# The phasor attention phase: output tile begun with three of four units, and the surplus matrix built in halves behind the phases

## The chip, the cores and the metric

The program runs on one core of one Trainium2 chip. The metric is device time of one execution in microseconds (us), lower is better. The kernel before takes 3089.39 us (median of three runs, 3087.33 to 3092.5).

## The reference, cut to what matters

The whole layer is attention of one kind (A), a feed-forward block (F), attention of another kind (B) and the same feed-forward block, each added to its input. The change touches only the first, on `x` of 8 rows, 1024 tokens, 256 features:

```python
x = x + attn_a(layernorm(x), Wk, Wv, Wo, gate, freqs)

def attn_a(x, Wk, Wv, Wo, gate, freqs):            # H, D = 16, 64; HD = 1024
    k_real = (x @ Wk).reshape(B, T, H, D)
    v = (x @ Wv).reshape(B, T, H, D).astype(complex64)
    k = exp(1j * (k_real * 10.0))
    rotors = exp(1j * (t[:, None, None] * freqs))[None]
    out_pos = real(cumsum(v * rotors, axis=1) * conj(rotors)) / sqrt(t + 1)
    k_shifted = roll(k, 1, axis=1).at[:, 0].set(0.0)
    out_assoc = real(cumsum(v * conj(k_shifted), axis=1) * k) / sqrt(t + 1)
    out = out_pos * gate[:, 0] + out_assoc * gate[:, 1]
    return out.reshape(B, T, HD) @ Wo
```

## The kernel before, in words

`build_layer` runs four phases one after the other, each in a block of its own with a barrier between: A, F, B, F. Only `phase_a` is changed. It walks over 8 batch rows (a "pass" each, the first and the last unrolled, the others in a loop), and in each over 8 **units** c = 0..7, a unit being 128 of the 1024 hidden features for all 1024 tokens. Units are numbered n = 8b + c through the phase.

Each engine has its own instruction list, written by hand, and runs it in order. Semaphores join them. For a unit n the work is:

- **TensorE** (PE) computes the phases' argument `u` (`project_u`, L627, 8 matmul records into `a_pu`) and `v` in two halves (`project_v`, L635, 4 records each into `a_pv`). An fp32 matmul is two records. It works ahead: in slot n it makes v of unit n+1 and u of unit n+2.
- **ScalarE** (ACT) in `front`: rounds u (L523, out `a_rnd`), then takes abs and two sines of the fraction (L525, L530, L531).
- **VectorE** (DVE) in `step`, 11 passes over the unit: products (L403 `even`, L408 `odd`), four scans (L414, L415), turns (L434, L444) and `fraction(n+1)` (L355), which needs the next unit's L523.
- **GpSimd** (POOL) in `post`, five passes (L268, L271, L277, L282, L285) that put the unit into `a_out[:, c]`; the last one signals `unit_done`. After units 1 and 2 it also makes the next row's means and scales.
- **TensorE** again, `project_out` (L658): 4 units are a **half row** of the hidden features. When units 0 to 3 are there, the four slots c = 4..7 each make two output tiles of 128 tokens, from a diagonal matmul with x (L670), for the first two slots two matmuls with the surplus matrix `fold` (L672), and four matmuls with `a_out` (L674). Units 4 to 7 are multiplied in slots c = 0..3 of the next pass. Before each pair it waits for `unit_done` of all four units. ScalarE scales the two tiles into `a_xr` (L538), SyncE stores them and loads the next row's x.

The order inside a TensorE slot is: first half of v, `project_out`, second half of v, u of unit n+2. So whatever `project_out` waits for, the second half of v and u wait too, and VectorE's L408 and L355 behind them.

The **surplus matrix** `fold` is needed since the scans run over pairs of neighbouring tokens: the sum of the earlier token of a pair holds the later one's term too. What is too much is linear in that token's x, and is added back with the opposite sign through a fixed 256x256 product of Wv, a scale per feature (`kap`) and Wo. It is built once, in the first pass, by `correction`: in slot 2 TensorE transposes `wv` (L648) in four groups into `a_py` and `a_pt`, ScalarE copies them scaled (L547, 8 copies) into the upper half of `a_out`; in slot 3 TensorE multiplies by `wo` (L655, 32 records) and ScalarE copies the two results (L551). On ScalarE, `correction(c)` stands ahead of `front` in its slot; ScalarE's other work there is sums of squares for the next row (`token_vars`, L497, 8 in slot 2) and normalising (L507).

```python
                def batch(b, first=False, last=False):     # ScalarE
                    for c in range(NC):
                        if first:
                            correction(c)
                        if not (last and c == NC - 1):
                            front(NC * b + c + 1, (c + 1) % NC, used=c >= 1 or not first)
```

## Time and profile before

| what | value |
|---|---|
| median of 3 runs | 3089.39 us (3087.33 to 3092.5) |
| the profiled execution | 3088.43 us, of which the span is 3086.6 us |
| mean granted TensorE clock | 0.961 of full |
| busy over the span: PE, DVE, ACT, POOL | 89%, 61%, 65%, 42% |
| phase A | from 0 to about 935 us |
| feed-forward 1, attention B, feed-forward 2 | to about 1560, 2480, 3087 us |

The span is what the profiler covers from the first to the last instruction. A row of the time line says when a group of instructions begins, how long it lasts, the engine, the line, output and inputs, how many there are, and in square brackets how long the engine was idle before it and what ended that. Since each engine runs in order, idle time of the engine that is busy nearly all of a phase is what a change can take away; idle time of another one costs only where its work is late for the first.

### The profile page before, as it was taken

Reading aid. Unit: us, or ns where it says so; the run is one execution under the profiler, and the core shown is the slowest. Engines: PE = TensorE matmul, PEld = TensorE weight load, DVE = VectorE, ACT = ScalarE, POOL = GpSimd, SP = SyncE. Lnnn points to the kernel's source line nnn. Section 1 sums busy time; section 2 is a strip of 40 time slices with the busy share of each in tenths; the row PEclk is TensorE's granted clock in tenths of the full one; section 3 lists DMA queues with packets and bytes.
Section 4 is the critical chain, followed back from the end, with each engine's and each line's share of the span. In section 5 each row is a group of like instructions: output and inputs, shape, how many; then the busy total and the mean of one; then the engine's idle time right before and its main releaser. Section 6 shows DMA issues by size and latency. Waiting matters only on the chain. (4 is left out here: it accounts for less than half of the span.)

```text
span 3086.6 us, 56032 instructions
## 1 busy us (share of the span) xinstructions
PE 2737.3 (89%) x20897; PEld 1237.3 (40%) x20897; DVE 1871.6 (61%) x2420; ACT 2021.0 (65%) x2650; POOL 1281.7 (42%) x786
## 2 busy tenths in 40 slices
PE   2799999998997999854999999989999999889997
PEld 1455555555563444321333333333333332244443
DVE  8899999999993444455455554544445441145434
ACT  6454555445434565532989897988989999745564
POOL 3788998989882112044414141313223120022110
PEclk7899999999998999967999999999999999989999
DMA  2010010001003121125445454554453636232112
GB/s 82 1 34 28 23 38 27 27 27 41 14 14 117 36 73 41 55 81 110 56 98 95 95 95 90 90 105 83 77 116 63 112 68 123 48 98 73 47 41 69
DMA packets 164064, 201.38 MB, mean 65 GB/s; under 512 B 16504, under 2 KB 118272, under 8 KB 163840
## 3 DMA queue, kind: packets, MB, share of 16 engines
q1 hardware_dynamic: 163840, 198.25, 28.8%
q8 instruction: 158, 2.59, 0.4%
q14 instruction: 66, 0.54, 0.1%
HBM read 139.49 MB, written 58.72 MB: 64 GB/s over the span
## 5 line engine op out<-in xcount | busy, mean ns | idle before, releaser
L1870 ACT ACTIVATE b_pr<-b_ps 128x1024 f32<-128x1024 f32 x1024 | 1000.1, 1035 | 175.6 <-PE b_ps L1889 170.1
L1889 PE MATMUL b_ps<-b_st 128*32 128x512 bf16 x8192 | 615.5, 383 | 55.2 <-ACT b_pr L1870 26.2
L1955 PE MATMUL b_acc<-b_pr,b_vaug 128*32 128x512 f32 x4096 | 532.8, 595 | 3.6 <-DVE b_osb L1758 3.3
L1889 PEld LDWEIGHTS b_ps<-b_st 128*32 128x32 bf16 x8192 | 179.6, 96 | 616.4 <-ACT b_pr L1870 363.7
L1257 PE MATMUL f_po<-f_s,f_w 128*128 128x512 f32 x768 | 356.8, 607 | 9.7 <-DVE f_xr L1042 5.9
L1030 DVE TENSOR_TENSOR f_turned<-f_cs,f_s 128x1024 f32<-128x1024 f32 x96 | 119.3, 1243 | 364.3 <-ACT f_cs L1159 359.3
L635 PE MATMUL a_pv<-a_xnT,a_wv 128*128 128x512 f32 x512 | 252.5, 617 | 52.5 <-DVE a_mem L403 39.4
L1123 ACT ACTIVATE f_h<-f_po,f_b 128x512 f32<-128x512 f32 x192 | 131.9, 687 | 220.2 <-PE f_po L1257 220.2
L1586 POOL TENSOR_TENSOR b_SQ<-b_A 128x1024 f32<-128x1024 f32 x32 | 66.7, 2084 | 482.8 <-DVE b_A L1683 482.8
L627 PE MATMUL a_pu<-a_xnT,a_wk 128*128 128x512 f32 x512 | 236.6, 605 | 29.7 <-DVE a_frac L355 23.7
L674 PE MATMUL a_py<-a_wo,a_out 128*128 128x256 f32 x960 | 229.2, 382 | 0.0
L1257 PEld LDWEIGHTS f_po<-f_s,f_w 128*128 128x128 f32 x768 | 142.0, 192 | 216.1 <-issue 161.9
L525 ACT ACTIVATE a_rnd<-a_frac 128x1024 f32<-128x1024 f32 x64 | 67.7, 1057 | 196.0 <-DVE a_frac L355 196.0
L674 PEld LDWEIGHTS a_py<-a_wo,a_out 128*128 128x128 f32 x960 | 184.6, 192 | 25.8
L523 ACT ACTIVATE a_rnd<-a_pu,a_cst 128x1024 f32<-128x1024 f32 x64 | 71.1, 1111 | 164.9 <-PE a_pu L627 164.9
L1265 PE MATMUL f_po<-f_h,f_w 128*128 128x512 f32 x384 | 175.5, 600 | 2.4 <-PEq L1248 2.0
L1955 PEld LDWEIGHTS b_acc<-b_pr,b_vaug 128*32 128x32 f32 x4096 | 125.2, 110 | 110.7 <-DVE b_osb L1758 6.7
L635 PEld LDWEIGHTS a_pv<-a_xnT,a_wv 128*128 128x128 f32 x512 | 96.7, 195 | 164.9 <-issue 85.0
L277 POOL TENSOR_TENSOR a_out<-a_mem,a_trig_k 128x1024 f32<-128x1024 f32 x64 | 139.6, 2182 | 54.7 <-DVE a_mem L415 54.7
L627 PEld LDWEIGHTS a_pu<-a_xnT,a_wk 128*128 128x128 f32 x512 | 99.1, 195 | 156.0 <-issue 129.4
L268 POOL TENSOR_TENSOR a_turn_c<-a_mem,a_trig_t 128x1024 f32<-128x1024 f32 x64 | 151.6, 2369 | 18.5 <-DVE a_mem L415 18.5
L414 DVE TENSOR_TENSOR_SCAN a_po<-a_mem,a_po 128x512 f32<-128x512 f32 x128 | 156.6, 1223 | 2.2
(261 smaller groups left out, 4552.9 us busy)
## 6 DMA issues: line engine op xcount, KB each, us to landing
b_st<-b_scratch SPq DMA_DIRECT2D x512, 128.0 KB, 7.3
b_scratch<-b_parts SPq DMA_DIRECT2D x32, 768.0 KB, 5.1
f_xl<-x SPq DMA_DIRECT2D x16, 1024.0 KB, 5.5
f_xr<-x SPq DMA_DIRECT2D x16, 1024.0 KB, 6.9
a_xl<-in_L_attn_a_x_dram SPq DMA_DIRECT2D x16, 512.0 KB, 4.5
x<-a_xr SPq DMA_DIRECT2D x32, 256.0 KB, 2.2
x<-f_xr SPq DMA_DIRECT2D x8, 1024.0 KB, 4.5
b_xl<-x SPq DMA_DIRECT2D x8, 1024.0 KB, 9.0
```

The source lines that it names most:

```text
L268: nc.gpsimd.tensor_tensor(halves(turn_c[:]), pair_of(s, 0), halves(cos_t[:, c, :]), ALU.mult).then_inc(turned, 1)
L277: nc.gpsimd.tensor_tensor(halves(o), pair_of(s, 2), of_tokens(cos_k[:, s, :]), ALU.mult).then_inc(turned, 1)
L414: nc.vector.tensor_tensor_scan(po[:, 1, :], mem[:, s, i, 1, :], po[:, 1, :], 0.0, ALU.add, ALU.add).then_inc(sin_scanned, 1)
L627: i = nc.tensor.matmul(pu[:, h * 512:(h + 1) * 512], wk_sb[:, k, c * P:(c + 1) * P], xnT[:, k, h * 512:(h + 1) * 512], start=k == 0, stop= ...
L635: i = nc.tensor.matmul(pv[:, h * 512:(h + 1) * 512], wv_sb[:, k, c * P:(c + 1) * P], xnT[:, k, h * 512:(h + 1) * 512], start=k == 0, stop= ...
L674: i = nc.tensor.matmul(o, out[:, c, t * P:(t + 1) * P], wo_sb[:, c, :], start=False, stop=c == c0 + HC - 1)
L1123: nc.scalar.activation(h1[:, x, m, h * HT:(h + 1) * HT], p, ACT.Gelu, bias=b1_sb[:, m:m + 1]).then_inc(act_done, 1)
L1257: q = nc.tensor.matmul(po[:, (at + t) % RING, :], w1_sb[:, f, m * P:(m + 1) * P], S[k][:, x, f, h * HT:(h + 1) * HT], start=f == 0, stop=f ...
L1265: q = nc.tensor.matmul(po[:, (at + h) % RING, :], w2_sb[:, f, :], h1[:, x, f, h * HT:(h + 1) * HT], start=f == 0, stop=f == KD - 1)
L1870: nc.scalar.activation(pr[:, 4 * (blk % 2) + j, :], ps[:, j % 2, :], ACT.Exp, scale=SC).then_inc(S["probs_done"], 1)
L1889: x = nc.tensor.matmul(o[r:r + 32], w[:, r:r + 32], v, start=start, stop=stop, skip_group_check=True)
L1955: x = nc.tensor.matmul(acc[32 * j:32 * j + 32, h * 512:(h + 1) * 512], vaug[:, kt, c:c + 32], pr[:, 4 * (kt % 2) + j, h * 512:(h + 1) * 51 ...
```

## The change

In `project_out`, the first pair of tiles of each half row (g = 0) now waits only for three units, and the wait for the fourth stands directly ahead of the first tile's last matmul. That is done in slot 4 and slot 0 of each pass. In the first pass, ScalarE does `front` ahead of the surplus matrix's work. TensorE makes the transposes at the end of slot 2, behind u of unit 4, and the product in two halves, into two banks: one between the halves of v in slot 3, the other at the end of slot 3. ScalarE's `token_vars` for row 1 waits until the scaled copies are done (both use `a_pt`), and GpSimd waits for both halves before it writes unit 4.

```diff
--- before.py
+++ after.py
@@ -273,7 +273,7 @@
                     if free is not None:
                         pool.wait_ge(wo_psum, free)
                     if isinstance(n, int) and n == HC:
-                        pool.wait_ge(fold_m, 1)
+                        pool.wait_ge(fold_m, KD)
                     nc.gpsimd.tensor_tensor(halves(o), pair_of(s, 2), of_tokens(cos_k[:, s, :]), ALU.mult).then_inc(turned, 1)
                     if end:
                         return
@@ -491,6 +491,8 @@
                 def token_vars(b):
 
                     act.wait_ge(mean_done, b + 1)
+                    if isinstance(b, int) and b == 1:
+                        act.wait_ge(fold_s, NC)
                     for t in range(NT):
                         if t >= 2:
                             act.wait_ge(vsum_done, NT * b + t - 1)
@@ -546,16 +548,16 @@
                             bank = pt if i // 2 % 2 else py
                             nc.scalar.activation(folded(i), bank[:, i % 2 * D:(i % 2 + 1) * D], ACT.Copy, scale=kap[:, i:i + 1]).then_inc(fold_s, 1)
                     if c == 3:
-                        act.wait_ge(fold_m, 1)
                         for k in range(KD):
-                            nc.scalar.activation(fold[:, k, :], py[:, k * D:(k + 1) * D], ACT.Copy).then_inc(fold_done, 1)
+                            act.wait_ge(fold_m, k + 1)
+                            nc.scalar.activation(fold[:, k, :], (pt if k else py)[:, 0:D], ACT.Copy).then_inc(fold_done, 1)
 
                 def batch(b, first=False, last=False):
                     for c in range(NC):
+                        if not (last and c == NC - 1):
+                            front(NC * b + c + 1, (c + 1) % NC, used=c >= 1 or not first)
                         if first:
                             correction(c)
-                        if not (last and c == NC - 1):
-                            front(NC * b + c + 1, (c + 1) % NC, used=c >= 1 or not first)
                         if c >= HC:
                             project_out(2 * NG * b + c - HC, c - HC)
                         elif not first:
@@ -636,29 +638,33 @@
                                              xnT[:, k, h * 512:(h + 1) * 512], start=k == 0, stop=k == KD - 1)
                     i.then_inc(v_psum, 1)
 
-                def correction(c):
-                    if c == 2:
-                        pe.wait_ge(xsum_done, 2 * NT)
-                        for g in range(NC // 2):
-                            if g >= 2:
-                                pe.wait_ge(fold_s, 2 * g - 2)
-                            bank = pt if g % 2 else py
-                            for i in (2 * g, 2 * g + 1):
-                                for k in range(KD):
-                                    x = nc.tensor.transpose(bank[:, i % 2 * D + k * P:i % 2 * D + (k + 1) * P],
-                                                            wv_sb[:, k, i * P:(i + 1) * P], ident[:])
-                            x.then_inc(fold_t, 1)
-                    if c == 3:
-                        pe.wait_ge(fold_s, NC)
-                        for k in range(KD):
-                            for i in range(NC):
-                                x = nc.tensor.matmul(py[:, k * D:(k + 1) * D], folded(i)[:, k * P:(k + 1) * P], wo_sb[:, i, :],
-                                                     start=i == 0, stop=i == NC - 1)
-                        x.then_inc(fold_m, 1)
+                def correction():
+
+                    pe.wait_ge(xsum_done, 2 * NT)
+                    for g in range(NC // 2):
+                        if g >= 2:
+                            pe.wait_ge(fold_s, 2 * g - 2)
+                        bank = pt if g % 2 else py
+                        for i in (2 * g, 2 * g + 1):
+                            for k in range(KD):
+                                x = nc.tensor.transpose(bank[:, i % 2 * D + k * P:i % 2 * D + (k + 1) * P],
+                                                        wv_sb[:, k, i * P:(i + 1) * P], ident[:])
+                        x.then_inc(fold_t, 1)
+
+                def correction_half(k):
+
+                    pe.wait_ge(fold_s, NC)
+                    bank = pt if k else py
+                    if k:
+                        pe.wait_ge(vsum_done, 2 * NT)
+                    for i in range(NC):
+                        x = nc.tensor.matmul(bank[:, 0:D], folded(i)[:, k * P:(k + 1) * P], wo_sb[:, i, :],
+                                             start=i == 0, stop=i == NC - 1)
+                    x.then_inc(fold_m, 1)
 
                 def project_out(k, g, units, c0, x_loads, free):
 
-                    pe.wait_ge(unit_done, units)
+                    pe.wait_ge(unit_done, units - 1 if g == 0 else units)
                     pe.wait_ge(xr_loaded, x_loads)
                     if free:
                         pe.wait_ge(wo_done, k)
@@ -671,6 +677,8 @@
                         for f in range(KD if c0 == 0 and t < NJ else 0):
                             nc.tensor.matmul(o, xnT[:, f, T2 + t * P:T2 + (t + 1) * P], fold[:, f, :], start=False, stop=False)
                         for c in range(c0, c0 + HC):
+                            if g == 0 and j == 0 and c == c0 + HC - 1:
+                                pe.wait_ge(unit_done, units)
                             i = nc.tensor.matmul(o, out[:, c, t * P:(t + 1) * P], wo_sb[:, c, :], start=False, stop=c == c0 + HC - 1)
                     i.then_inc(wo_psum, 1)
 
@@ -685,8 +693,8 @@
                             project_out(2 * NG * b + g, g, NC * b + HC, 0, loads, not first or g >= 1)
                         elif not first:
                             project_out(2 * NG * (b - 1) + NG + c, c, NC * b, HC, 32, True)
-                        if first:
-                            correction(c)
+                        if first and c == 3:
+                            correction_half(0)
                         if not (last and c == NC - 1):
                             project_v(n + 1, (c + 1) % NC, 1)
                         if c == NC - 2 and not last:
@@ -694,6 +702,10 @@
                             pe.wait_ge(xt_done, 4 * (b + 1) + 4)
                         if not (last and c >= NC - 2):
                             project_u(n + 2, (c + 2) % NC)
+                        if first and c == 2:
+                            correction()
+                        if first and c == 3:
+                            correction_half(1)
 
                 pe.wait_ge(id_done, 2)
                 pe.wait_ge(freq_loaded, 16)
```

How the instruction lists move, at the three places that matter. First TensorE in the first pass, slots 2 and 3. Before:

```order
L635 MATMUL a_pv<-a_xnT,a_wv 128x512 [waits a_even_done]
L648 MATMUL a_py<-a_ident,a_wv 128x128 [waits a_xsum_done]
L648 MATMUL a_pt<-a_ident,a_wv 128x128 x4
L635 MATMUL a_pv<-a_xnT,a_wv 128x512 [waits a_odd_done]
L627 MATMUL a_pu<-a_xnT,a_wk 128x512 [waits a_frac_done]
L635 MATMUL a_pv<-a_xnT,a_wv 128x512 [waits a_even_done]
L655 MATMUL a_py<-a_wo,a_out 128x256 [waits a_fold_s]
L655 MATMUL a_py<-a_wo,a_out 128x256 x15
L635 MATMUL a_pv<-a_xnT,a_wv 128x512 [waits a_odd_done]
L627 MATMUL a_pu<-a_xnT,a_wk 128x512 [waits a_frac_done]
```

and now, from the second half of v in slot 2 on:

```order
L637 MATMUL a_pv<-a_xnT,a_wv 128x512 [waits a_odd_done]
L629 MATMUL a_pu<-a_xnT,a_wk 128x512 [waits a_frac_done]
L650 MATMUL a_py<-a_ident,a_wv 128x128 [waits a_xsum_done]
L650 MATMUL a_pt<-a_ident,a_wv 128x128 x4
L637 MATMUL a_pv<-a_xnT,a_wv 128x512 [waits a_even_done]
L661 MATMUL a_py<-a_wo,a_out 128x256 [waits a_fold_s]
L661 MATMUL a_py<-a_wo,a_out 128x256 x7
L637 MATMUL a_pv<-a_xnT,a_wv 128x512 [waits a_odd_done]
L629 MATMUL a_pu<-a_xnT,a_wk 128x512 [waits a_frac_done]
L661 MATMUL a_pt<-a_wo,a_out 128x256 [waits a_vsum_done,a_fold_s]
```

The transposes went from between the halves of v to behind u, and half of the 16 matmuls went from between the halves of v to behind u of the next slot.

Second, ScalarE in the same slots. Before:

```order
L547 ACTIVATE a_out<-a_py,a_kap 128x256 [waits a_fold_t,a_kap_done]
L523 ACTIVATE a_rnd<-a_pu,a_cst 128x1024 [waits a_trig_done,a_u_psum]
L525 ACTIVATE a_rnd<-a_frac 128x1024 [waits a_frac_done]
L497 ACTIVATE a_pt,a_sm<-a_xl,a_sm 128x256 [waits a_mean_done]
L551 ACTIVATE a_fold<-a_py 128x256 [waits a_fold_m]
```

and now:

```order
L525 ACTIVATE a_rnd<-a_pu,a_cst 128x1024 [waits a_trig_done,a_u_psum]
L527 ACTIVATE a_rnd<-a_frac 128x1024 [waits a_frac_done]
L549 ACTIVATE a_out<-a_py,a_kap 128x256 [waits a_fold_t,a_kap_done]
L499 ACTIVATE a_pt,a_sm<-a_xl,a_sm 128x256 [waits a_fold_s,a_mean_done]
L525 ACTIVATE a_rnd<-a_pu,a_cst 128x1024 [waits a_trig_done,a_u_psum]
L527 ACTIVATE a_rnd<-a_frac 128x1024 [waits a_frac_done]
L553 ACTIVATE a_fold<-a_py 128x256 [waits a_fold_m]
L553 ACTIVATE a_fold<-a_pt 128x256 [waits a_fold_m]
L509 ACTIVATE a_xl<-a_xl,a_sm 128x256 [waits a_rstd_done]
```

The rounding of unit 3 now precedes the scaled copies, and that of unit 4 the copies of the product; but the sums of squares are now held by the scaled copies, and stand ahead of the rounding of unit 4.

Third, TensorE at slot 4, where a half row's first pair begins. Before:

```order
L670 MATMUL a_py<-a_xr,a_diag 128x256 [waits a_fold_done,a_xr_loaded,a_unit_done]
L672 MATMUL a_py<-a_fold,a_xnT 128x256 x2
L674 MATMUL a_py<-a_wo,a_out 128x256 x4
L670 MATMUL a_py<-a_xr,a_diag 128x256
L635 MATMUL a_pv<-a_xnT,a_wv 128x512 [waits a_odd_done]
```

and now:

```order
L676 MATMUL a_py<-a_xr,a_diag 128x256 [waits a_fold_done,a_xr_loaded,a_unit_done]
L678 MATMUL a_py<-a_fold,a_xnT 128x256 x2
L682 MATMUL a_py<-a_wo,a_out 128x256 x3
L682 MATMUL a_py<-a_wo,a_out 128x256 [waits a_unit_done]
L676 MATMUL a_py<-a_xr,a_diag 128x256
L637 MATMUL a_pv<-a_xnT,a_wv 128x512 [waits a_odd_done]
```

Six matmuls (twelve records) now stand ahead of the wait for the fourth unit, which ends up at the seventh.

## Rows read from the trace of the kernel before

**Rows 1.** windows view, phase A; busy us (count) of PE, PEld, DVE, ACT, POOL, then PEclk, DMA
```profile
0.00:935.00 935.00, 805.58 (x2609) 488.93 (x2609) 879.20 (x759) 465.54 (x780) 781.60 (x394) 0.97 0.09 31
```

**Rows 2.** waits view, VectorE, 60 to 935 us; us in total, times, longest
```profile
DVE a_po L408 <- PE a_pv L635: 17.1, 8, 3.6
DVE a_frac L355 <- ACT a_rnd L523: 14.6, 9, 7.3
```

**Rows 3.** time line of VectorE, passes 1 and 3
```profile
230.56 1.21 DVE L355 SCALAR_TENSOR_TENSOR a_frac<-a_rnd,a_pu 128x1024 f32<-128x1024 f32 x1
...
243.30 1.21 DVE L355 SCALAR_TENSOR_TENSOR a_frac<-a_rnd,a_pu 128x1024 f32<-128x1024 f32 x1
...
252.32 1.29 DVE L408 SCALAR_TENSOR_TENSOR a_po<-a_pv,a_gates,a_trig_t 128x1024 f32<-128x1024 f32 x1 [1.93 <-PE a_pv L635]
...
284.37 1.22 DVE L355 SCALAR_TENSOR_TENSOR a_frac<-a_rnd,a_pu 128x1024 f32<-128x1024 f32 x1 [0.57 <-ACT a_rnd L523]
...
463.55 1.29 DVE L408 SCALAR_TENSOR_TENSOR a_po<-a_pv,a_gates,a_trig_t 128x1024 f32<-128x1024 f32 x1 [3.61 <-PE a_pv L635]
```

**Rows 4.** time line of TensorE, then of GpSimd, slot 4 of pass 1
```profile
240.08 1.98 PE L635 MATMUL a_pv<-a_xnT,a_wv 128*128 128x512 f32 x4 [1.29 <-DVE a_mem L403]
244.28 0.67 PE L670 MATMUL a_py<-a_xr,a_diag 128*128 128x256 f32 x2 [2.22 <-POOL a_out L285]
...
241.68 2.34 POOL L285 TENSOR_TENSOR a_out<-a_out,a_turn_v 128x1024 f32<-128x1024 f32 x1
```

**Rows 5.** waits view, TensorE, 160 to 935 us
```profile
PE a_py L670 <- POOL a_out L285: 16.5, 14, 2.2
```

**Rows 6.** windows view, slot 4 of pass 3; columns as in rows 1
```profile
449.00:454.00 5.00, 2.16 (x5) 0.89 (x6) 5.00 (x6) 0.50 (x1) 4.92 (x3) 1.00 0.15 52
454.00:457.50 3.50, 3.50 (x10) 2.76 (x10) 3.46 (x4) 3.15 (x3) 3.34 (x2) 0.53 0.00 0
```

**Rows 7.** page, costliest groups: TensorE's weight loads at L674
```profile
L674 PEld LDWEIGHTS a_py<-a_wo,a_out 128*128 128x128 f32 x960 | 184.6, 192 | 25.8
```

**Rows 8.** time line of VectorE, first pass
```profile
107.44 1.22 DVE L355 SCALAR_TENSOR_TENSOR a_frac<-a_rnd,a_pu 128x1024 f32<-128x1024 f32 x1 [3.41 <-ACT a_rnd L523]
...
127.60 1.22 DVE L355 SCALAR_TENSOR_TENSOR a_frac<-a_rnd,a_pu 128x1024 f32<-128x1024 f32 x1 [7.33 <-ACT a_rnd L523]
```

**Rows 9.** time line of TensorE, first pass
```profile
102.55 0.60 PE L648 MATMUL a_py<-a_ident,a_wv 128*128 128x128 f32 x4
...
109.92 3.44 PE L635 MATMUL a_pv<-a_xnT,a_wv 128*128 128x512 f32 x4 [4.39 <-DVE a_po L408]
...
116.97 1.99 PE L635 MATMUL a_pv<-a_xnT,a_wv 128*128 128x512 f32 x4 [0.18 <-DVE a_mem L403]
118.79 7.07 PE L655 MATMUL a_py<-a_wo,a_out 128*128 128x256 f32 x32
130.07 3.60 PE L635 MATMUL a_pv<-a_xnT,a_wv 128*128 128x512 f32 x4 [4.21 <-DVE a_po L408]
...
137.13 1.98 PE L635 MATMUL a_pv<-a_xnT,a_wv 128*128 128x512 f32 x4
139.62 0.70 PE L670 MATMUL a_py<-a_xr,a_diag 128*128 128x256 f32 x2 [0.51 <-POOL a_out L285]
```

**Rows 10.** time line of ScalarE, first pass
```profile
106.29 1.11 ACT L523 ACTIVATE a_rnd<-a_pu,a_cst 128x1024 f32<-128x1024 f32 x1
...
111.78 0.46 ACT L497 ACTIVATE a_pt<-a_xl,a_sm 128x256 f32<-128x256 f32 x1
...
115.62 0.19 ACT L497 ACTIVATION_READ_ACCUMULATOR a_pt<-a_xl,a_sm 128x1 f32 x1
...
126.44 1.12 ACT L523 ACTIVATE a_rnd<-a_pu,a_cst 128x1024 f32<-128x1024 f32 x1
...
131.94 1.57 ACT L507 ACTIVATE a_xl<-a_xl,a_sm 128x256 f32<-128x256 f32 x3
```

**Rows 11.** time line of GpSimd, first pass
```profile
145.21 2.18 POOL L277 TENSOR_TENSOR a_out<-a_mem,a_trig_k 128x1024 f32<-128x1024 f32 x1 [0.87 <-DVE a_mem L415]
```

## The prediction

> **What bounds the kernel now.** I split the span by phase first. In phase A VectorE is busy 879.2 of 935 us, GpSimd 781.6, TensorE 805.6, ScalarE 465.5 [rows 1]. The four phases are separated by barriers and only A is changed, so what VectorE gains in A should reach the end one for one. VectorE's waits come next: 17.1 us in 8 waits for the second half of v, and 14.6 us in 9 for the rounding of u [rows 2]. Without a wait one unit takes 243.30 - 230.56 = 12.74 us [rows 3].
>
> The time line places the waits. In pass 1 VectorE stands 1.93 us ahead of `odd` of unit c = 5, in pass 3 it is 3.61 us [rows 3]. The eight waits are 1.93 in passes 1, 2 and 4, 3.6 in passes 3, 5 and 6, and about 0.26 in passes 0 and 7: 5.8 + 10.8 + 0.5 = 17.1. Who is late? TensorE finishes the first half of v and then stands 2.22 us for GpSimd's last operation on unit 3 (241.68 + 2.34 = 244.02) before the first output tile begins at 244.28 [rows 4]; the second half of v is queued behind it. So a wait for GpSimd reaches VectorE through TensorE's queue. Such waits ahead of L670 sum to 16.5 us in 14 [rows 5]; only those in slot 4 matter, those in slot 0 are short.
>
> In pass 3 the same wait costs more, since TensorE's granted clock, full in the 5 us before it, in which TensorE was busy for only 2.16 us, is 0.53 in the 3.5 us after it, that is near its lower level of 1.2 GHz [rows 6]. The extra price is 3.61 - 1.93 = 1.68 us.
>
> The first pass has two stalls of its own: 3.41 us before L355 at 107.44 and 7.33 us at 127.60 [rows 8]. ScalarE's rounding of u of unit 3 stands behind the 8 scaled copies (it begins at 106.29), and that of unit 4 behind the copy of the product (126.44) [rows 10], which ended 7.07 us of matmuls [rows 9].
>
> **Part 1: the tile begun early.** Half of v begun at 116.97 lets the next instruction start at 118.79, 1.82 us later [rows 9]. In slot 4 of pass 1 TensorE is therefore free at 240.08 + 1.82 = 241.90. The product of 16 matmuls took 7.07 us, 0.44 each; six of them are 2.6 us [rows 9]. They end at 244.5, behind 244.28, when the fourth unit was seen before [rows 4]. So the new wait should be over when it is reached, by 0.2 us, and TensorE's whole stream moves up by 244.28 - 241.90 = 2.38 us. VectorE could have run `odd` at 252.32 - 1.93 = 250.39; its input now comes at 252.32 - 2.38 = 249.94. That stall goes. What is late next is TensorE again: it streams without a gap through slots 4 to 6 and the transposes, and VectorE waits 0.57 us for the rounding at 284.37 [rows 3]. VectorE alone would be there 1.93 + 0.57 = 2.50 us (a little more with waits too short to show) earlier, TensorE 2.38. The lesser one counts: **2.38 us a pass**, and about 0.1 us of that late wait stays.
>
> Six passes (1 to 6) give 6 x 2.38 = 14.3 us. In the three passes with the clock fall I also take back 1.68 each, **5.0 us**, because what preceded the fall was the idle time that goes; a shorter stop of 1.29 us stays ahead of the first half of v [rows 4], and behind that one the clock was still full [rows 6]. In pass 7 GpSimd makes no scales and is earlier, so little is to be had: 0.26 + about 0.1 = 0.4 us. In slot 0 four matmuls are brought forward, and VectorE does not wait there: nothing. The second tile, ScalarE's L538, the stores of x and SyncE's loads, all move up with TensorE and nobody waits for them.
>
> The added wait stands between a tile's matmuls, ahead of a matmul whose stationary operand is the fourth unit itself. Its price isn't in the trace. From below 0: halves of v with a wait that is already met follow the matmuls before them with no gap shown, as at 137.13 [rows 9]. From above one weight load, 192 ns [rows 7], in 7 passes 1.3 us. I take 0, the nearer row. The Trainium skill ("TensorE: Matmul & The Clock Gate", section "Architectural detail") states that TensorE's queue pulls weight loads ahead of matmuls in flight; a load that has to wait for its operand could not be pulled, which speaks for the upper end and would make the sum 1.3 us less.
>
> **Part 2: the first pass.** ScalarE rounds unit 3 with nothing ahead, so the 3.41 us stall goes and L355 is at 104.03. Everything up to u of unit 4 follows VectorE and moves up 3.4 us: TensorE's half of v at 106.5, and u ends near 116.8 - 3.4 = 113.4 (it ended just before 116.97) [rows 9]. Now the transposes and copies begin. From the first transpose to ScalarE being free it took 106.29 - 102.55 = 3.74 us: 117.1. The sums of squares, which had 111.78 to 115.81, 4.03 us, follow: 121.2 [rows 10]. Only then is unit 4 rounded, and from there to L355 it is 127.60 - 126.44 = 1.16 us [rows 8, 10]: 122.3. VectorE could be there at 104.03 + 12.74 = 116.8. **The 7.33 us stall becomes 5.5 us**: the copies were hidden behind ScalarE's idle time and are now in its way.
>
> The next one is new. ScalarE's second copy of `fold` waits for the second half product, which TensorE makes behind v and u. From L355 at 122.3: 130.07 - 127.60 = 2.47 to the half of v, 137.13 - 130.07 = 7.06 for it and u, 7.07 / 2 = 3.53 for the half product [rows 8, 9], 0.3 for one copy, 1.57 for three normalisings, 1.16 to L355 [rows 10]: 16.1 us where a unit wants 12.74, **a new stall of 3.4 us**. TensorE's first output tile comes after the half product (135.4) and a half of v: 137.2, where it was 139.62 [rows 9]. From there to the next pass TensorE is again the one to be waited for, so the first pass gains 139.62 - 137.2 = **2.4 us**. GpSimd gets its scales about 2 us later than before, but was ready for that tile at 139.6 behind VectorE's old stalls, and unit 3 now follows an L355 that is 5.3 us earlier; its wait for both half products (135.4) is over long before it writes unit 4 (before at 145.21 [rows 11]).
>
> The bounds of this term: the halves of v and u at 109.92 and 130.07 ran in part at the lower clock (3.27 and 3.44 us to the next instruction, against 1.82). Were both full, 1.6 us each would come on top: 5.7. Were the half product at the lower level, 3.5 us more are on the path: a loss of 1.1 us.
>
> **The sum.** 14.3 + 5.0 + 0.4 + 2.4 = 22.1 us off 3088.43 gives 3066.3. The median of the runs is 0.96 us above the profiled execution, so I forecast **3067 us**.
>
> **Rivals.**
> 1. *The clock falls stay*, moved to another idle time such as the 1.29 us one. The sum loses 5.0: 3072 us. For it: only three of six equal passes fell, so the fall does not hang on this idle time alone. Against: each was right behind it. The Trainium skill ("TensorE: Matmul & The Clock Gate", section "What's actually happening") says that the clock is throttled by default and activity releases it; by that rule less idle time should mean fewer falls, which is the forecast's side. Chance 0.12.
> 2. *The first pass gives nothing or loses*, as ScalarE's queue carries the transposes' copies, the sums and both product copies ahead of roundings. With -1.1 and 1.3 for the waits, the sum is 14.3 + 5.0 + 0.4 - 1.1 - 1.3 = 17.3: 3072 us. Chance 0.12.
> 3. *The wait only moves.* If GpSimd ends the fourth unit some 2.4 us later against VectorE than now, TensorE stands ahead of the seventh matmul as long as it did ahead of the first; then the change doesn't do what it says, and only 2.4 + 0.4 are left: 3086.6 us, no change. Against it: GpSimd's order and its inputs from VectorE are the same in passes 1 to 6, and it is idle in each pass (781.6 of 935 busy). Chance 0.05.
> 4. *Slower: the clock falls oftener.* TensorE works six matmuls, stops again, and the clock falls both for the tiles and for v behind them, in all seven passes. Eleven more falls than today's three at 1.68 are 18.5 us, with a first pass that loses 1.1: 3089.4 + 19.6 = 3109 us. It decides where the stop ahead of the seventh matmul is over about 1.3 us, since stops of 1.29 stay at full clock now and that of 2.22 fell in half of the passes. I reckon with none at all. Chance 0.03.
>
> **How the numbers follow.** Forecast 0.68, rivals 0.12, 0.12, 0.05, 0.03. A measurement here tells some 0.2%, 6.2 us, from no change. Forecast and rivals 1 and 2 are all faster by more, 0.92; rival 3 is within, 0.05; rival 4 is slower, 0.03. The range: upward rivals 1 and 2 with both their ends, 22.1 - 5.0 - 3.5 - 1.3 = 12.3 off: 3077. Downward 3.3 for a first pass at full clock, and some 3 us because the other phases' clock and the number of falls vary between executions (the runs spread over 5 us): 3061.
>
> **What the changed profile should show.** No stall over 0.3 us of VectorE at `odd` of unit 5; six passes each shorter by 2.4 us, three of them by 4.1; in slot 4 no idle time of TensorE ahead of the first tile and none or a tenth or two ahead of its last matmul; full granted clock there in all passes. In the first pass no stall before L355 of unit 3, 5.5 us before that of unit 4, 3.4 us before that of unit 5, and the end of phase A some 22 us earlier. A stall of over 1 us at `odd` of unit 5, or one that appears in another slot, would prove part 1 wrong; stalls in the first pass that sum to over 11 us would prove part 2 wrong.

## The result, and the profile after

The changed kernel takes 3067.18 us (median of 4 runs, 3059.23 to 3069.34); the kernel before, in runs beside it, 3090.32 us (4 runs, 3087.33 to 3092.5). The ratio is 0.9921 with a 95% interval of 0.9901 to 0.9942: 0.8% faster, and the interval is clear of 1.

The profiled execution of the change took 3059.23 us, the lowest of its runs, so the two profiled spans differ by 29.2 us, more than the medians. Where phase A ends can be read from the row of the table load with which ScalarE begins the next phase (the source view of that line; minimum, median and maximum in ns, then first and last start). Before, and after:

```profile
L1098 ACT ACT_TABLE_LOAD  x2: 1283/1283/1283, 934.9 to 2697.2; - x2
```

```profile
L1110 ACT ACT_TABLE_LOAD  x2: 1283/1283/1283, 913.2 to 2671.5; - x2
```

Phase A ends at 913.2 us instead of 934.9, **21.7 us earlier**. The other 7.5 us are in phases whose code is unchanged: from that row to the end it was 2151.7 us before and 2144.2 us in this execution. Experiment 9 below runs the same kernel again and finds 2153.6 us there, so 7.5 us is within what one kernel's executions differ by there. I judge everything below by phase A, and mostly by where VectorE begins its last addition but one (L467 in most of the kernels): 921.96 us before, 900.25 us after.

VectorE's waits in phase A after (waits view, as [rows 2]). The row for the second half of v is gone:

```profile
DVE a_frac L355 <- ACT a_rnd L525: 12.3, 9, 5.6
```

Its stalls behind 60 us in order of time (time line, as [rows 3, 8]): the first two are in slots 2 and 3 of the first pass, the others stand at the last rounding of passes 0, 1 and 2, and those of passes 3 to 6 are like the last one:

```profile
122.36 1.22 DVE L355 SCALAR_TENSOR_TENSOR a_frac<-a_rnd,a_pu 128x1024 f32<-128x1024 f32 x1 [5.62 <-ACT a_rnd L525]
...
139.58 1.22 DVE L355 SCALAR_TENSOR_TENSOR a_frac<-a_rnd,a_pu 128x1024 f32<-128x1024 f32 x1 [4.38 <-ACT a_rnd L525]
...
178.06 1.22 DVE L355 SCALAR_TENSOR_TENSOR a_frac<-a_rnd,a_pu 128x1024 f32<-128x1024 f32 x1 [0.18 <-ACT a_rnd L525]
...
280.57 1.22 DVE L355 SCALAR_TENSOR_TENSOR a_frac<-a_rnd,a_pu 128x1024 f32<-128x1024 f32 x1 [0.51 <-ACT a_rnd L525]
...
382.88 1.22 DVE L355 SCALAR_TENSOR_TENSOR a_frac<-a_rnd,a_pu 128x1024 f32<-128x1024 f32 x1 [0.32 <-ACT a_rnd L525]
```

From 178.06 to 280.57 a pass is 102.51 us, the next one 102.31. Before, the same two stretches were 104.79 and 104.76 us (179.58 to 284.37 [rows 3] to 389.13), and 106.5 us in the three passes with a fall of the clock. Slot 4 of pass 2, TensorE and then GpSimd (time line, as [rows 4]):

```profile
341.05 1.98 PE L637 MATMUL a_pv<-a_xnT,a_wv 128*128 128x512 f32 x4 [1.29 <-DVE a_mem L403]
342.87 0.59 PE L676 MATMUL a_py<-a_xr,a_diag 128*128 128x256 f32 x2
...
345.89 0.59 PE L676 MATMUL a_py<-a_xr,a_diag 128*128 128x256 f32 x2
...
342.59 2.35 POOL L285 TENSOR_TENSOR a_out<-a_out,a_turn_v 128x1024 f32<-128x1024 f32 x1
```

TensorE goes from v to the first tile at 342.87, 1.82 us after v began, while GpSimd's last operation on the fourth unit runs until 344.94. The seven matmuls of the tile take 345.89 - 342.87 = 3.02 us, 0.43 each, with no idle time ahead of the last: it begins at about 342.87 + 6 x 0.43 = 345.45, 0.5 us behind GpSimd's end, so the added wait was met when TensorE came to it. The granted clock in slot 4 of pass 3 (windows view, columns as [rows 1]) is full where it was 0.53 before [rows 6], and so it is from 140 to 900 us throughout:

```profile
442.00:445.00 3.00, 1.71 (x5) 0.87 (x5) 3.00 (x4) 1.11 (x1) 2.78 (x3) 1.00 0.28 87
445.00:450.00 5.00, 5.00 (x24) 4.25 (x23) 4.96 (x5) 2.01 (x2) 4.84 (x3) 1.00 0.00 0
```

The first pass, TensorE and then ScalarE (time lines, as [rows 9, 10]):

```profile
106.39 3.32 PE L637 MATMUL a_pv<-a_xnT,a_wv 128*128 128x512 f32 x4 [3.70 <-DVE a_po L408]
109.51 4.00 PE L629 MATMUL a_pu<-a_xnT,a_wk 128*128 128x512 f32 x8
113.34 0.60 PE L650 MATMUL a_py<-a_ident,a_wv 128*128 128x128 f32 x4
...
124.84 3.78 PE L637 MATMUL a_pv<-a_xnT,a_wv 128*128 128x512 f32 x4 [3.35 <-DVE a_po L408]
128.42 4.78 PE L629 MATMUL a_pu<-a_xnT,a_wk 128*128 128x512 f32 x8
133.04 3.62 PE L661 MATMUL a_pt<-a_wo,a_out 128*128 128x256 f32 x16
...
138.21 0.59 PE L676 MATMUL a_py<-a_xr,a_diag 128*128 128x256 f32 x2
```

```profile
121.24 1.09 ACT L525 ACTIVATE a_rnd<-a_pu,a_cst 128x1024 f32<-128x1024 f32 x1
...
136.69 0.38 ACT L553 ACTIVATE a_fold<-a_pt 128x256 f32<-128x256 f32 x1 [9.62 <-PE a_pt L661]
...
138.44 1.10 ACT L525 ACTIVATE a_rnd<-a_pu,a_cst 128x1024 f32<-128x1024 f32 x1
```

The half product that begins at 133.04 is what ScalarE's second copy waits for (136.69), and the rounding of unit 5 stands behind that copy and three normalisings at 138.44. Both halves of v above, behind idle times of 3.70 and 3.35 us, last longer than the 1.98 us of a full clock (3.32 and 3.78).

### The profile page after: what moved, and what is told of

The parts are those of the page before. It is cut to its first block and busy times, and to the rows that moved or that the text cites. A ratio compares the mean times of both kernels' runs of the same rounds, so it can differ in the third digit from the quotient of the medians.

```text
span 3057.4 us, 56040 instructions
## 1 busy us (share of the span) xinstructions
PE 2724.2 (89%) x20897; PEld 1237.4 (40%) x20897; DVE 1869.9 (61%) x2420; ACT 2020.9 (66%) x2650; POOL 1278.9 (42%) x786
## 5 line engine op out<-in xcount | busy, mean ns | idle before, releaser
L629 PE MATMUL a_pu<-a_xnT,a_wk 128*128 128x512 f32 x512 | 238.6, 610 | 29.2 <-DVE a_frac L355 23.2
L682 PE MATMUL a_py<-a_wo,a_out 128*128 128x256 f32 x960 | 226.8, 379 | 0.0
L682 PEld LDWEIGHTS a_py<-a_wo,a_out 128*128 128x128 f32 x960 | 182.4, 190 | 24.8
L271 POOL TENSOR_TENSOR a_turn_c<-a_turn_c,a_turn_s 128x1024 f32<-128x1024 f32 x64 | 151.4, 2365 | 9.6 <-POOL a_turn_c L268 8.4
```

The costliest lines, as they stand in the source:

```text
L271: nc.gpsimd.tensor_tensor(turn_c[:], turn_c[:], turn_s[:], ALU.add).then_inc(added, 1)
L629: i = nc.tensor.matmul(pu[:, h * 512:(h + 1) * 512], wk_sb[:, k, c * P:(c + 1) * P], xnT[:, k, h * 512:(h + 1) * 512], start=k == 0, stop= ...
L682: i = nc.tensor.matmul(o, out[:, c, t * P:(t + 1) * P], wo_sb[:, c, :], start=False, stop=c == c0 + HC - 1)
```

## The experiments

Each is told with its edit, what was expected, what was measured, and what follows. "The point" is where VectorE begins its last addition but one: 921.96 us before, 900.25 in the change. Where no number of runs is given, the kernel was run once, and the reading rests on its trace.

**1. The early tile alone.** The kernel before with the two edits of `project_out`:

```diff
-                    pe.wait_ge(unit_done, units)
+                    pe.wait_ge(unit_done, units - 1 if g == 0 else units)
...
+                            if g == 0 and j == 0 and c == c0 + HC - 1:
+                                pe.wait_ge(unit_done, units)
```

> The early tile alone, the surplus matrix as before. I measure phase A by where VectorE begins its last addition but one (921.96 us in the trace before, 900.25 in that of the change). My theory: the early tile is worth 2.4 us in each of passes 1 to 6, 1.7 more in each pass in which the clock fell, and 0.4 in pass 7, so that point comes at 901 to 903 and the time is about 3070. Rival 1 (the falls stay): 906 to 908, about 3075. Rival 3 (the wait only moves): 919 or later, no change.

Measured: 3067.68 us (4 runs), ratio to before 0.9925 (0.9908 to 0.9943); the point at 901.10. VectorE's stalls at unit 4 and at the end of pass 1:

```profile
127.76 1.22 DVE L355 SCALAR_TENSOR_TENSOR a_frac<-a_rnd,a_pu 128x1024 f32<-128x1024 f32 x1 [7.52 <-ACT a_rnd L523]
...
281.31 1.22 DVE L355 SCALAR_TENSOR_TENSOR a_frac<-a_rnd,a_pu 128x1024 f32<-128x1024 f32 x1 [0.31 <-ACT a_rnd L523]
```

So 20.9 of the 21.7 us are the early tile's, within what was expected: 0.6 in the first pass (its last rounding is at 178.98, it was at 179.58), 19.7 in passes 1 to 6, the rest in pass 7. The first pass keeps its long stall (7.5 us here, 7.3 before), and the stalls at `odd` are gone from all passes. Rivals 1 and 3 fall, and with them rival 4: the clock is full in all of passes 1 to 7.

**2. The surplus matrix's new order alone.** The change with `project_out` as before.

> The surplus matrix's new order alone, all waits for four units as before. My theory: the first pass gains 1.5 us as in the trace of the change (stalls of 5.6 and 4.4 us in place of 3.4 and 7.3), passes 1 to 7 stall as before, 1.9 or 3.6 us each; VectorE's last addition but one at 920.5, give or take 1.7 for each clock fall more or fewer than three; time within 3 us of before. A rival that gives the rework the larger share of the 22 us would put that point below 915.

Measured: 3086.68 us (10 runs), ratio 0.9996 (0.9982 to 1.0011): no difference that can be told. The point is at 919.17, 2.8 us earlier than before, all of it in the first pass. The stalls at `odd` are back, again 1.9 us in three passes and 3.6 us in three, though not the same three:

```profile
138.32 1.22 DVE L355 SCALAR_TENSOR_TENSOR a_frac<-a_rnd,a_pu 128x1024 f32<-128x1024 f32 x1 [3.12 <-ACT a_rnd L525]
...
249.56 1.29 DVE L408 SCALAR_TENSOR_TENSOR a_po<-a_pv,a_gates,a_trig_t 128x1024 f32<-128x1024 f32 x1 [1.96 <-PE a_pv L637]
...
356.02 1.29 DVE L408 SCALAR_TENSOR_TENSOR a_po<-a_pv,a_gates,a_trig_t 128x1024 f32<-128x1024 f32 x1 [3.62 <-PE a_pv L637]
```

The new stall at unit 5 is here (3.12 us), with L355 at 138.32; in the change it was 4.38. The 1.26 us between are the clock: v and u behind the second wait took 131.78 - 124.84 = 6.94 us here and 8.20 in the change, with the same work before them. So the rework is the small part, worth 0.85 us on top of the early tile (901.10 against 900.25), and by itself 2.8 us, or 1.5 with the clock of the change.

**3. The early tile in slot 4 only.** As 1, with `and c0 == 0` in both conditions.

> The early tile in slot 4 only; slot 0 waits for all four units as before, the surplus matrix as before. My theory: VectorE never waits for slot 0's tiles, so this is the early tile alone (901 to 903 for VectorE's last addition but one). A rival: TensorE's idle time in slot 0 counts as well, for the clock or later in the pass; then it is 1 us or more later than with both.

Measured: the point at 900.88, 3064.58 us in its one run. In experiment 1 it was at 901.10, and a pass is 102.33 us in both, so slot 0's share is nothing. The whole gain is taken in slot 4, where TensorE is the one waited for.

**4. Idle time filled, nothing brought forward.** The kernel before with five extra matmuls in slot 4, between the wait for three units and the wait for the fourth:

```diff
-                    pe.wait_ge(unit_done, units)
+                    pe.wait_ge(unit_done, units - 1 if g == 0 and c0 == 0 else units)
...
+                        if g == 0 and c0 == 0 and j == 0:
+                            for _ in range(5):
+                                nc.tensor.matmul(o, diag[:, t, :], xr[:, t, :], start=True, stop=True)
+                            pe.wait_ge(unit_done, units)
```

> The kernel before, but while TensorE waits for the fourth unit in slot 4 it repeats the tile's first matmul (diagonal by x) five times, which changes nothing in the result and brings nothing forward: 2.2 us of work in the place of 2.2 us of idle time. If the clock falls come from that idle time, they vanish: full granted clock in slot 4 of all passes, stalls of about 1.9 us in all six passes and none of 3.6, VectorE's last addition but one near 917, 5 us earlier than in the trace before. If they come from elsewhere (rival 1), some passes still show 3.6 us. If the five matmuls end late they would add up to 0.2 us a pass.

Measured: the point at 918.50, the time 3083.55 us. The stalls in passes 0, 1 and 3:

```profile
149.10 1.29 DVE L408 SCALAR_TENSOR_TENSOR a_po<-a_pv,a_gates,a_trig_t 128x1024 f32<-128x1024 f32 x1 [1.64 <-PE a_pv L635]
...
253.53 1.29 DVE L408 SCALAR_TENSOR_TENSOR a_po<-a_pv,a_gates,a_trig_t 128x1024 f32<-128x1024 f32 x1 [1.75 <-PE a_pv L635]
...
462.68 1.29 DVE L408 SCALAR_TENSOR_TENSOR a_po<-a_pv,a_gates,a_trig_t 128x1024 f32<-128x1024 f32 x1 [1.72 <-PE a_pv L635]
```

All six passes 1 to 6 now show 1.72 to 1.75 us, none 3.6, and the clock is full in all of them. That no pass falls, where three of six fell before and three of six in experiment 2, says that the falls came from TensorE's idle time, as the forecast had it. The point is 1.5 us later than expected. In passes 0 and 7, which waited only 0.25 us, the extra matmuls are themselves late (1.64 us of stall each), 2.8 us in the two; the six others give back 0.2 us each. I had overlooked the two.

**5. The price of a wait that is met.** The change with such a wait ahead of every L682 matmul:

```diff
+                            else:
+                                pe.wait_ge(unit_done, units - 1 if g == 0 and j == 0 else units)
```

> The changed kernel with a wait that is already met ahead of each of the four L682 matmuls of every tile, 8 a slot instead of one in two slots. It prices the wait that part 1 put between a tile's matmuls. My theory: it costs nothing, VectorE's last addition but one stays near 900.3 us. The rival from the weight load (192 ns exposed at each): slots 4 to 6, where TensorE is the one waited for, get 24 x 0.19 = 4.6 us longer, 7 passes some 32 us: that point near 932 us, and L682's matmuls 0.62 us apart instead of 0.43.

Measured: the time 3060.45 us; a pass is still 102.3 us long (378.24 to 480.56), and the tiles in pass 2 are as tight as without the waits. The row of PEld is TensorE's weight loads for the matmuls in the row below it:

```profile
338.24 0.59 PE L676 MATMUL a_py<-a_xr,a_diag 128*128 128x256 f32 x2
...
339.32 1.70 PEld L684 LDWEIGHTS a_py<-a_wo,a_out 128*128 128x128 f32 x8
...
339.53 1.89 PE L684 MATMUL a_py<-a_wo,a_out 128*128 128x256 f32 x8
...
341.26 0.59 PE L676 MATMUL a_py<-a_xr,a_diag 128*128 128x256 f32 x2
```

The second tile begins 3.02 us after the first, as in the change: the waits cost nothing, and the weight load of 192 ns that made the upper bound is not exposed. The Trainium skill ("TensorE: Matmul & The Clock Gate", section "Architectural detail") says that loads are pulled ahead of matmuls in flight. This trace agrees, for matmuls that stand behind a wait which is already met: their eight loads run from 339.32 to 341.02, the matmuls from 339.53 to 341.42. Of a wait ahead of a tile's last matmul that is not yet met no run here has a trace. But the point was at 895.64, 4.6 us *earlier* than in the change, and all of it in the first pass, ahead of the first of the added waits:

```profile
106.39 1.98 PE L637 MATMUL a_pv<-a_xnT,a_wv 128*128 128x512 f32 x4 [3.70 <-DVE a_po L408]
108.21 3.60 PE L629 MATMUL a_pu<-a_xnT,a_wk 128*128 128x512 f32 x8
...
123.14 1.98 PE L637 MATMUL a_pv<-a_xnT,a_wv 128*128 128x512 f32 x4 [3.35 <-DVE a_po L408]
124.96 3.60 PE L629 MATMUL a_pu<-a_xnT,a_wk 128*128 128x512 f32 x8
...
133.56 0.59 PE L676 MATMUL a_py<-a_xr,a_diag 128*128 128x256 f32 x2
```

The v of slot 2 hands over after 1.82 us here and after 3.12 us in the change, that of slot 3 after 1.82 and 3.58. The added waits all come later than these rows of v and u, so they are not the cause. The clock was the suspect, which asked for experiments 8 and 9.

**6. The sums of squares in ScalarE's idle time.** In the first pass they write their unused product to a spare SBUF tile, `aside`, instead of the bank `a_pt`, and stand ahead of the scaled copies:

```diff
-                    if isinstance(b, int) and b == 1:
-                        act.wait_ge(fold_s, NC)
...
-                        nc.scalar.activation(spare(t), xl[:, t, :], ACT.Square, bias=nmean[:, t:t + 1],
+                        nc.scalar.activation(aside[:, t % 2, :] if isinstance(b, int) and b == 1 else spare(t), xl[:, t, :], ACT.Square, bias=nmean[:, t:t + 1],
...
+                        if first and c == VARS_AT:
+                            token_vars(b + 1)
                         if first:
                             correction(c)
...
-                        if c == VARS_AT and not last:
+                        if c == VARS_AT and not last and not first:
                             token_vars(b + 1)
```

> The changed kernel, but in the first pass ScalarE's sums of squares write their unused product into SBUF instead of the bank that the transposes use, and stand ahead of the scaled copies, in ScalarE's idle time. If the 5.6 us stall before L355 of unit 4 comes from the sums that stand behind the copies (4.0 us of it), L355 comes at 118.4 instead of 122.4 (stall 1.6) and the next half of v at 121.4, with TensorE hardly idle before it. The first tile of slot 4 then begins near 131.8 to 134, where it was 138.2, and VectorE's last addition but one at 894 to 896 (900.25 in the change). A rival, that the copies and the transposes are the cause, leaves it at 900.

Measured: VectorE's L355 (L356 in this kernel) of unit 4 at 118.24, the first tile at 131.65, the point at 893.52, each just under what was expected; the time 3060.44 us:

```profile
118.24 1.22 DVE L356 SCALAR_TENSOR_TENSOR a_frac<-a_rnd,a_pu 128x1024 f32<-128x1024 f32 x1 [1.49 <-ACT a_rnd L524]
...
133.02 1.22 DVE L356 SCALAR_TENSOR_TENSOR a_frac<-a_rnd,a_pu 128x1024 f32<-128x1024 f32 x1 [1.95 <-ACT a_rnd L524]
...
121.33 1.88 PE L638 MATMUL a_pv<-a_xnT,a_wv 128*128 128x512 f32 x4
...
126.48 3.62 PE L662 MATMUL a_pt<-a_wo,a_out 128*128 128x256 f32 x16
...
131.65 0.59 PE L677 MATMUL a_py<-a_xr,a_diag 128*128 128x256 f32 x2
```

The stall of 5.6 us falls to 1.5, with the transposes at 113.34 as in the change. So 4.1 us of it came from the sums that the change had put between the copies and the rounding. Of the 6.56 us by which the first tile is earlier, 124.84 - 121.33 = 3.51 are TensorE's idle time ahead of this half of v, which is gone. The other 3.05 are the clock: with no stop ahead of them, v and u take 126.48 - 121.33 = 5.15 us where they took 8.20.

**7. Both half products between the halves of v**, and then this together with 6.

```diff
                         if first and c == 3:
                             correction_half(0)
+                            correction_half(1)
...
-                        if first and c == 3:
-                            correction_half(1)
```

> The changed kernel, but the second half product directly behind the first, between the halves of v in slot 3. TensorE is idle there for 3.35 us in the trace of the change, as long as a half product takes. If the 4.4 us stall before L355 of unit 5 comes from the half product behind u, it vanishes; the half of v then follows a busy TensorE at full clock, the first tile begins near 134 instead of 138.2, and VectorE's last addition but one is at about 896. A rival, that the second half product is hidden behind other work anyway, leaves 900.

> Both of the last two edits in one. TensorE is then the one waited for in slots 3 and 4, so the two gains don't add: I expect L355 of unit 4 at 118.4, that of unit 5 without a stall, the first tile near 132, and VectorE's last addition but one at about 894, 6 us less than in the change; the time near 3061. If the gains add, 890; if either edit's gain is lost, 896.

Measured for the halves together: the point at 895.75, the time 3062.84 us, and no stall at unit 5. TensorE works through where it stood 3.35 us in the change, so the clock does not fall there either. The stall of 4.38 us thus had two causes that this run takes away together, and experiment 8 tells them apart:

```profile
117.86 3.62 PE L661 MATMUL a_py<-a_wo,a_out 128*128 128x256 f32 x16
121.47 3.69 PE L661 MATMUL a_pt<-a_wo,a_out 128*128 128x256 f32 x16
124.99 1.88 PE L637 MATMUL a_pv<-a_xnT,a_wv 128*128 128x512 f32 x4
...
133.71 0.59 PE L676 MATMUL a_py<-a_xr,a_diag 128*128 128x256 f32 x2
```

Measured for both edits: the point at 891.80, the time 3062.76 us (4 runs, 3060.89 to 3063.94), ratio to before 0.9915 (0.9890 to 0.9939). Of VectorE's waits in the first pass behind 60 us one over 1 us is left, for a half of v behind the second half product:

```profile
125.00 1.29 DVE L409 SCALAR_TENSOR_TENSOR a_po<-a_pv,a_gates,a_trig_t 128x1024 f32<-128x1024 f32 x1 [1.26 <-PE a_pv L638]
...
169.81 1.22 DVE L356 SCALAR_TENSOR_TENSOR a_frac<-a_rnd,a_pu 128x1024 f32<-128x1024 f32 x1 [0.42 <-ACT a_rnd L524]
```

The gains don't add, as expected: 6.7 and 4.5 apart, 8.5 together. Of the 8.5 us, 1.7 is a clock that did not fall ahead of the transposes (they began at 111.64, not 113.34), which neither edit touches. Without that the two together are worth 6.8 us, no more than experiment 6 alone, which already leaves TensorE no idle time there. This trace has the shortest phase A of all, but its median of the time is 4.4 us under the change's with runs that overlap and were not taken side by side, so the time alone doesn't show a gain over the change.

**8. Idle time filled in the first pass.** The change with 8 matmuls where TensorE waited in slot 2 and 7 in slot 3, behind the first half product, their result unused:

```diff
+                def busy(n):
+                    for _ in range(n):
+                        x = nc.tensor.matmul(py[:, D:2 * D], diag[:, 0, :], xr[:, 0, :], start=True, stop=True)
+                    return x
...
+                    if not k:
+                        x = busy(7)
...
+                        if first and c == 2:
+                            pe.wait_ge(xr_loaded, 32)
+                            busy(8)
```

> The changed kernel with idle matmuls (diagonal by x into the free half of a_py, result never used) in TensorE's two waits of the first pass: eight where it waited 3.70 us before the half of v in slot 2, seven where it waited 3.35 us in slot 3. Nothing is brought forward. In the trace of the change the first tile of slot 4 began at 138.2, in the run with the met waits at 133.6, with the same order of work there but full granted clock throughout. If that difference is the clock alone, it is now full in the first pass in any execution, the first tile begins at 133.6 and VectorE's last addition but one at 895.6. If the difference had another cause (the met waits themselves), it stays at 138 and 900, or later by what the idle matmuls add.

Measured: the first tile at 133.57, the point at 895.71, the time 3065.23 us. The windows over v and u in slots 2 and 3 (columns as [rows 1]), then VectorE's two stalls:

```profile
105.50:110.00 4.50, 4.25 (x12) 1.91 (x12) 4.46 (x5) 2.82 (x3) 3.50 (x2) 1.00 0.00 0
...
124.80:128.40 3.60, 3.60 (x10) 1.52 (x8) 3.60 (x4) 0.57 (x2) 3.60 (x2) 1.00 0.00 0
...
120.67 1.22 DVE L355 SCALAR_TENSOR_TENSOR a_frac<-a_rnd,a_pu 128x1024 f32<-128x1024 f32 x1 [3.92 <-ACT a_rnd L525]
...
134.94 1.22 DVE L355 SCALAR_TENSOR_TENSOR a_frac<-a_rnd,a_pu 128x1024 f32<-128x1024 f32 x1 [1.44 <-ACT a_rnd L525]
```

The useful work is placed as in the change, so of its stalls of 5.62 and 4.38 us the clock made 1.70 and 2.94; the half product behind u made the 1.44 that are left of the second.

**9. The change once more.**

> The changed kernel again, to see how far its first pass varies between executions. If the clock's falls in the first pass come and go, the first tile of slot 4 begins anywhere from 133.6 (no fall) to 138.2 (both falls reaching into u), while passes 1 to 6 stay at 102.3 to 102.5 us each. If the first pass is fixed, 138.2 again.

Measured: the first tile at 138.18, the point at 900.33, the time 3068.74 us. The same windows:

```profile
105.50:110.00 4.50, 3.59 (x5) 1.65 (x6) 4.46 (x5) 2.83 (x3) 3.49 (x2) 0.65 0.01 4
...
124.80:128.40 3.60, 3.55 (x4) 1.51 (x5) 3.57 (x4) 2.28 (x3) 3.52 (x2) 0.50 0.00 0
```

So the 4.6 us are the clock: 0.65 and 0.50 in the one, 1.00 in the other, with the same useful work in the same order. Both traces of the change show the falls, and that of experiment 5, whose first pass is the same program up to the first tile, shows none. And from the row of the next phase's table load (913.3) to the end of its span of 3066.9 us it took 2153.6 us:

```profile
L1110 ACT ACT_TABLE_LOAD  x2: 1283/1283/1283, 913.3 to 2677.7; - x2
```

## Why the prediction was right, point by point

The forecast was 3067 us, the median is 3067.18. That the two are 0.2 us apart is luck: the four runs spread over 10 us. What can be compared is phase A, 22.1 us forecast and 21.7 measured. By its steps:

- **The early tile, passes 1 to 6.** Predicted 14.3 + 5.0 = 19.3 us. From the last rounding of pass 0 to that of pass 6 it was 813.29 - 179.58 = 633.7 us before and is 792.13 - 178.06 = 614.1: 19.6 us. The stall at `odd` is gone in every pass, TensorE starts the tile 1.82 us after v, and what is late next is the rounding at the pass's end, as foretold. Two sizes differ. A pass without a fall gained 104.76 - 102.31 = 2.45 us, not 2.38: behind the stop, the first tile had taken 352.14 - 349.05 = 3.09 us in pass 2 before, where it takes 3.02 now. And of the late rounding's 0.57 us, 0.3 to 0.5 stay, not 0.1, while a wait of 0.16 us at `odd` in slot 6, too short for the list, went. The reading that TensorE streams without a gap through the transposes is also not exact: it stops there for ScalarE's copies twice, 0.33 and 0.76 us in pass 2 before, 0.21 and 0.76 now.
- **The clock's fall as part of the idle time's price.** A pass with a fall was 106.46 us long against 104.76, 1.7 more, so its 5.0 us were right, and experiment 4 shows the cause by itself: the falls vanish when the idle time is filled with useless work. That three of the six passes fell, and not one or five, was a property of the one trace that the sum was made from; in experiment 2 it was three again, not the same ones.
- **The added wait.** Taken at 0; 0 in experiment 5. The upper bound of one weight load did not arise, since the wait was met 0.5 us before its matmul's turn.
- **Pass 7.** Predicted 0.4; 108.67 us from the last rounding of pass 6 to the point before, 108.12 now: 0.55.
- **The first pass.** Predicted stalls of 5.5 and 3.4 us, measured 5.62 and 4.38; predicted gain 2.4 us, measured 1.5. The step that was off is the 7.06 us for v and u behind the second wait. I had taken it from the trace before, where u was at full clock; here v and u took 133.04 - 124.84 = 8.2 us, since the clock stayed low into u. The lower bound of this term (-1.1) was not reached. Its upper one (5.7) was too low: with a full clock the gain is 179.58 - 173.43 = 6.2 us (experiment 8). By its own rows the bound is even 2.4 + 1.45 + 1.62 = 5.5. What it lacked are steps that are each shorter than I put them: at full clock v and u take 128.40 - 123.14 = 5.26 us, not 7.06 - 1.62 = 5.44, L355 of unit 4 is at 120.67, not 120.85, and the half product and the half of v behind it take 0.2 us less together.
- **The size of the two parts.** Argued as 19.7 and 2.4 us; experiments 1 and 2 give 20.9 and 0.85 to 2.8. The sum gave the early tile nothing in the first pass, and it took 0.6 us there. The rework on top of it was worth about a third of what was forecast, nearer to rival 2's nothing than to the forecast. Two things that made it small were named beforehand and are shown in 6 and 8: the sums ahead of a rounding (4.1 us) and a half product on the path (1.4 us). The third, the larger share of the second stall, was in the prediction only as a bound: the clock, which fell behind both of TensorE's stops, 1.7 and 2.9 us. Each of these was measured with the others in place, so they are not terms of a sum.
- **The range, 3061 to 3077 us.** The median is in it, the profiled execution (3059.23 us) is just below. I had allowed 3 us for phases that the change does not touch; they moved by 9.4 us between two executions of the same kernel.

## What to carry to other kernels

Look for the wait that holds an in-order queue, then ask what stands behind it and not only what it waits for: in slot 4 VectorE did not wait for GpSimd, TensorE did, and VectorE's input stood behind it in TensorE's list. Beginning an accumulation with the parts that are there, and waiting only ahead of the last, cost nothing and took 20.9 us off. When one-off work is moved "behind" the critical work, check whose queue it then heads: here stalls of 3.4 and 7.3 us went and stalls of 5.6 and 4.4 us came. Placing the same sums in ScalarE's idle time (experiment 6) left 1.5 and 1.95 us.

## What the runs showed of the hardware

- TensorE's idle time costs twice: the stop itself and, in some executions, half the speed for what follows. The stop of 2.2 us ahead of the tile was followed by a fall in 3 of 6 passes before and in 3 of 6 in experiment 2, each 1.7 us more.
- The same stop of 3.70 us in the first pass stands in seven traces, those of the change and of experiments 2, 5, 6, 7 (both versions) and 9. It was followed by a granted clock of 0.62 to 0.75 from 105.5 to 110 us in five of them and by a full one in two, experiment 5 and the second version of 7. In these two TensorE's stop ahead of the half of v at 100.7 was 0.32 and 0.35 us, in four others 1.3; but in experiment 2 it was 0.41 us and the clock fell even so, a little later. What decides is open.
- Behind the stops that were filled with useless matmuls the clock did not fall in experiments 4 and 8: six passes of slot 4 in the one, both stops of the first pass in the other. It still fell in experiment 4 behind the stops of the first pass that were not filled.
- The phases behind A, in code that no experiment touched, took from 2144.2 us (the change's profile) to 2154.3 us (the second version of experiment 7); the change run again had 2153.6. I did not look into why. The 9.4 us between the two traces of one kernel are over 40% of the change's effect, so two spans of one execution each can't be compared to better than some 0.3%.
